# Two cleared sums take the last six blocks' rows of a sparse layer, and the other result rows are loaded meanwhile

## The reference

```python
top_w, top_idx = jax.lax.top_k(scores, TOP_K)          # TOP_K = 4, 16 experts
top_w = top_w / jnp.sum(top_w, axis=-1, keepdims=True)
g = jnp.einsum('bsh,khe->bske', x, gate_proj)          # h = 256, e = 224
u = jnp.einsum('bsh,khe->bske', x, up_proj)
act = jax.nn.silu(g) * u
out = jnp.einsum('bske,keh->bskh', act, down_proj)
sel = jnp.take_along_axis(out, top_idx[..., None], axis=2)
return jnp.sum(sel * top_w[..., None], axis=2)         # and x + this is the output
```

## Time and profile before

| | |
|---|---|
| median of three runs | 856.86 us |
| profiled execution, first to last instruction | 859.4 us |
| PE busy | 775.1 us, 90% |
| DVE busy | 554.2 us, 64% |
| ACT busy | 384.4 us, 45% |
| POOL busy | 238.3 us, 28% |
| mean granted TensorE clock | 0.956 |

### The profile page before, as it was taken

The page is one execution under the profiler, slowest core; times in us unless marked ns, Lnnn a source line. Parts: engine busy times, 40 slices in busy tenths (PEclk is TensorE's granted clock), DMA queues, the critical chain, the costliest instruction groups (busy, mean ns, idle before and its releaser), DMA issues. The chain is left out here.

```text
span 859.4 us, 15356 instructions
## 1 busy us (share of the span) xinstructions
PE 775.1 (90%) x5288; PEld 566.7 (66%) x5288; DVE 554.2 (64%) x1291; ACT 384.4 (45%) x847; POOL 238.3 (28%) x296
## 2 busy tenths in 40 slices
PE   6899878999999999997778999989989888999995
PEld 2455546878998999993335655555555537888884
DVE  3799946533432222223987999899996357888854
ACT  2466534332321111110334766666675407888860
POOL 2344420520000000004641433444431421434340
PEclk8999988999999999999899999899999798999999
DMA  9465441390289999836610001010125119999817
GB/s 337 176 245 223 189 153 56 94 405 16 78 296 387 388 345 316 304 137 158 203 34 2 25 11 45 25 51 31 46 82 208 56 42 347 411 396 393 336 56 251
DMA packets 57104, 158.03 MB, mean 184 GB/s; under 512 B 7180, under 2 KB 36748, under 8 KB 51708
## 3 DMA queue, kind: packets, MB, share of 16 engines
q1 hardware_dynamic: 51700, 141.97, 45.5%
q0 software_dynamic: 5328, 15.08, 4.9%
HBM read 114.21 MB, written 42.81 MB: 183 GB/s over the span
## 5 line engine op out<-in xcount | busy, mean ns | idle before, releaser
L1271 PEld LDWEIGHTS ps<-f_xT,f_rg 128*128 128x128 f32 x920 | 113.4, 192 | 5.2 <-DMA f_rg<-w_routed 1.7
L1271 PE MATMUL ps<-f_xT,f_rg 128*128 128x128 f32 x920 | 113.9, 275 | 1.3 <-DMA f_rg<-w_routed 1.3
L1176 DVE TENSOR_TENSOR f_rhT<-f_gate,ps 128x256 f32<-128x256 f32 (+1 forms) x69 | 25.9, 376 | 117.2 <-ACT f_gate L981 73.0
L2078 ACT ACTIVATE b_PX<-ps 128x512 f32<-128x512 f32 x128 | 72.7, 597 | 46.3 <-PE ps L2313 44.7
L1811 DVE TENSOR_REDUCE b_smax<-ps 128x4 f32<-128x1024 f32 x64 | 77.9, 1217 | 15.7 <-PE ps L2289 15.4
L981 ACT ACTIVATE f_gate<-ps 128x256 f32<-128x256 f32 (+1 forms) x69 | 24.0, 348 | 134.2 <-PE ps L1271 134.2
L2606 POOL DMA_INDIRECT y<-f_ys,f_to x47 | 45.1, 959 | 81.7 <-DVE f_to L2684 78.2
L1285 PE MATMUL ps<-f_rd,f_rhT 128*128 128x256 f32 x230 | 62.3, 387 | 0.0
L2313 PE MATMUL ps<-b_Q,b_Cx 100*128 100x256 f32 x256 | 55.8, 327 | 6.3 <-ACT b_PX L2078 6.0
L2313 PEld LDWEIGHTS ps<-b_Q,b_Cx 100*128 100x128 f32 x256 | 41.9, 206 | 26.6 <-ACT b_PX L2078 12.2
L1583 POOL MEMSET b_half<- 128x1 f32 x1 | 0.1, 99 | 212.9 <-POOLq L69 212.9
(11 more groups left out here) (333 smaller groups left out, 1843.1 us busy)
## 6 DMA issues: line engine op xcount, KB each, us to landing
f_rg<-w_routed SPq DMA_DIRECT2D x23, 1280.0 KB
rows<-a_blank SPq DMA_DIRECT2D x16, 1152.0 KB, 7.0
f_rd<-w_routed SPq DMA_DIRECT2D x23, 640.0 KB, 5.5
f_rw<-w_ffn SPq DMA_DIRECT2D x19, 704.0 KB
rw<-w_ffn SPq DMA_DIRECT2D x16, 704.0 KB
later<-w_ffn SPq DMA_DIRECT2D x12, 704.0 KB
f_xs<-rows SPq DMA_DIRECT2D x31, 144.0 KB
f_yk<-y SPq DMA_DIRECT2D x8, 512.0 KB, 7.8
```

The costliest lines, as they stand in the source:

```text
L1271: mm = nc.tensor.matmul(ps[:, u % 4, k * P:(k + 1) * P], rg[b % R_SLOTS][:, off:off + P], xT[b % 2][:, c, :], start=(c == 0), stop=(c == C ...
L2078: nc.scalar.activation(PX[g % RING][:].rearrange("p c m -> p (c m)"), ps[:, RETS + G_TURN[g] % 2, :], ACT.Exp, scale=XSC).then_inc(turn_re ...
```

## The change

Layer 1's result tensor y grows by two sums of 1024 token rows each, with 128 rows beside each for rows that hold no token (SUM_ROWS1 = 1152). In layer 0's experts stage SP clears y's first 4096 rows (4096 KB) and the two sums (2304 KB) from a zero tile. The first 41 blocks of layer 1 scatter as before. The last six (ADDED1) compute another destination: the token's row in sum b % 2, or a row beside it. POOL scatters them with an add; from the third of the six on it first waits until the scatter two blocks earlier, to the same sum, has landed. SP waits for the first 41 scatters only, loads `yk`, then waits for the others and loads the two sums of each tile (`ya`, 256 KB each). PE adds all tiles' `yk` rows 0 and 1, then all tiles' `ya` rows, into the same PSUM banks; DVE does its two adds for all tiles, then the final ones. PE's filler matmuls at the end are gone.

```diff
+ADDED1 = 6
+SUMS1 = TOP1 * TOKENS + BLOCKS1 * P
+SUM_ROWS1 = TOKENS + P
...
@@ routed_experts, SP, in the loop over the loads of chunks 4 to 9
                 sp.dma_start(raw[j % W_SLOTS][:], w_shared[j]).then_inc(w_loaded[j % W_SLOTS], 16)
+                if j == SHARED_CHUNKS - 3:
+                    sp.wait_ge(zeros_set, 1)
+                    nothing = zeros[:].bitcast(F32)
+                    first = results_dram[0:TOP1 * TOKENS].rearrange("(p n) d -> p n d", p=P)
+                    sums = results_dram[SUMS1:SUMS1 + 2 * SUM_ROWS1].rearrange("(p n) d -> p n d", p=P)
+                    for to, n in ((first, TOP1 * TOKENS // P), (sums, 2 * SUM_ROWS1 // P)):
+                        sp.dma_start(to, bc(nothing, 1, n)).then_inc(results_cleared, 16)
...
+            sp.wait_ge(results_cleared, 32)
...
@@ sparse_experts, SP
             for n in range(Y_SLOTS):
-                sp.wait_ge(y_sent[n], 16 * ((BLOCKS1 + Y_SLOTS - 1 - n) // Y_SLOTS))
+                sp.wait_ge(y_sent[n], 16 * ((BLOCKS1 - ADDED1 + Y_SLOTS - 1 - n) // Y_SLOTS))
             per_tile = y_dram[0:TOP1 * TOKENS].rearrange("(k t p) d -> t p k d", k=TOP1, p=P)
             for t in range(TILES):
                 sp.dma_start(yk[t][:], per_tile[t]).then_inc(yk_loaded[t], 16)
+            for n in range(Y_SLOTS):
+                sp.wait_ge(y_sent[n], 16 * ((BLOCKS1 + Y_SLOTS - 1 - n) // Y_SLOTS))
+            sums = y_dram[SUMS1:SUMS1 + 2 * SUM_ROWS1].rearrange("(k n) d -> n k d", k=2)
+            for t in range(TILES):
+                sp.dma_start(ya[t][:], sums[t * P:(t + 1) * P]).then_inc(ya_loaded[t], 16)
...
@@ POOL
-                pool.indirect_dma_start(y_dram, bass.IndirectOffsetOnAxis(ap=to[b % A_SLOTS][:, 0:1], axis=0), ys[b % Y_SLOTS][:], None
-                                        ).then_inc(y_sent[b % Y_SLOTS], 16)
+                at = bass.IndirectOffsetOnAxis(ap=to[b % A_SLOTS][:, 0:1], axis=0)
+                if b < BLOCKS1 - ADDED1:
+                    pool.indirect_dma_start(y_dram, at, ys[b % Y_SLOTS][:], None).then_inc(y_sent[b % Y_SLOTS], 16)
+                    continue
+                if b >= BLOCKS1 - ADDED1 + 2:
+                    pool.wait_ge(y_sent[(b - 2) % Y_SLOTS], 16 * ((b - 2) // Y_SLOTS + 1))
+                pool.indirect_dma_start(y_dram, at, ys[b % Y_SLOTS][:], None, compute_op=ALU.add).then_inc(y_sent[b % Y_SLOTS], 16)
...
@@ DVE, address(b)
+                s, n = b % 2, b - BLOCKS1 + ADDED1
+                nc.vector.tensor_copy(token[s][:], at).then_inc(token_ready, 1)
+                nc.vector.tensor_scalar(unused[s][:], at, float(TOP1 * TOKENS), beside[:, s:s + 1], ALU.is_ge, ALU.mult).then_inc(token_ready, 1)
+                dve.wait_ge(token_ready, 3 * n + 2)
+                nc.vector.tensor_scalar(token[s][:], token[s][:], TOKENS - 1, None, ALU.bitwise_and).then_inc(token_ready, 1)
+                dve.wait_ge(token_ready, 3 * n + 3)
+                nc.vector.scalar_tensor_tensor(out=to[b % A_SLOTS][:], in0=token[s][:], scalar=float(SUMS1 + s * SUM_ROWS1), in1=unused[s][:],
+                                               op0=ALU.add, op1=ALU.max).then_inc(to_ready, 1)
...
@@ DVE, before the blocks: two more columns like `nowhere`; after them: the final add in a loop of its own
+            for s in range(2):
+                nc.vector.tensor_scalar(beside[:, s:s + 1], K[:, K_PAD:K_PAD + 1], float(SUMS1 + s * SUM_ROWS1 + TOKENS - TOP1 * TOKENS), None,
+                                        ALU.add).then_inc(nowhere_set, 1)
...
+            for t in range(TILES):
                 dve.wait_ge(whole_sum, t + 1)
                 dve.wait_ge(pair_sum, t + 1)
                 nc.vector.tensor_tensor(X[:, t, :], ps[:, t, 0:D], X[:, t, :], ALU.add).then_inc(x_added, 1)
...
@@ PE, the end
-            keep_busy(24)
             pe.wait_ge(y_kept, BLOCKS1)
-            for n in range(Y_SLOTS):
-                pe.wait_ge(y_sent[n], 16 * ((BLOCKS1 + Y_SLOTS - 1 - n) // Y_SLOTS))
-            keep_busy(30)
             for t in range(TILES):
                 pe.wait_ge(yk_loaded[t], 16)
                 for k in range(2):
-                    mm = nc.tensor.matmul(ps[:, t, 0:D], ident, yk[t][:, k], start=(k == 0), stop=(k == 1))
+                    nc.tensor.matmul(ps[:, t, 0:D], ident, yk[t][:, k], start=(k == 0), stop=False, skip_group_check=True)
+            for t in range(TILES):
+                pe.wait_ge(ya_loaded[t], 16)
+                for k in range(2):
+                    mm = nc.tensor.matmul(ps[:, t, 0:D], ident, ya[t][:, k], start=False, stop=(k == 1), skip_group_check=True)
                 mm.then_inc(pair_sum, 1)
```

More of the change, by code:

```diff
@@ L119, in decoder_kernel @@
             routed_experts(nc, "f0", w_shared0, w_routed0, rows0_dram, y0_dram, X, XN, xh, xl, K, KR, ps, logits0, dest0, wk0,
-                           raw0, w0_loaded, ctx_rows, ctx_dram, blank_ctx)
+                           raw0, w0_loaded, ctx_rows, ctx_dram, blank_ctx, y1_dram)
         eb1 = whole.enter_context(nc.sbuf_tensor("eb1", [P, MORE1], mybir.dt.int32))
@@ L776, in routed_experts @@
 def routed_experts(nc, tag, w_shared, w_routed, rows_dram, y_dram, X, XN, xh, xl, K, KR, ps, logits, dest, wk, raw, w_loaded,
-                   ctx_rows, ctx_dram, blank_ctx):
+                   ctx_rows, ctx_dram, blank_ctx, results_dram):
     ctx = ExitStack()
@@ L889, in routed_experts @@
         row_set = sem("row_set")
+        results_cleared = sem("results_cleared")
         blank_stored = sem("blank_stored")
@@ L2520, in sparse_experts @@
         nowhere = sb("nowhere", [P, BLOCKS1])
+        beside = sb("beside", [P, 2])
+        token = [sb(f"token{n}", [P, 1], mybir.dt.int32) for n in range(2)]
+        unused = [sb(f"unused{n}", [P, 1]) for n in range(2)]
+        ya = [sb(f"ya{t}", [P, 2, D]) for t in range(TILES)]
         yk = [sb(f"yk{t}", [P, TOP1, D]) for t in range(TILES)]
@@ L2542, in sparse_experts @@
         yk_loaded = [sem(f"yk_loaded{t}") for t in range(TILES)]
+        ya_loaded = [sem(f"ya_loaded{t}") for t in range(TILES)]
+        token_ready = sem("token_ready")
         half_sum = sem("half_sum")
@@ L2683, in address @@
                     dve.wait_ge(y_sent[b % Y_SLOTS], 16 * (b // Y_SLOTS))
-                nc.vector.tensor_tensor(to[b % A_SLOTS][:], pick[b % A_SLOTS][:, 1:2], nowhere[:, b:b + 1], ALU.min).then_inc(to_ready, 1)
+                at = pick[b % A_SLOTS][:, 1:2]
+                if b < BLOCKS1 - ADDED1:
+                    nc.vector.tensor_tensor(to[b % A_SLOTS][:], at, nowhere[:, b:b + 1], ALU.min).then_inc(to_ready, 1)
+                    return
+                s, n = b % 2, b - BLOCKS1 + ADDED1
[6 more added lines that the diff above has]
+                                               op0=ALU.add, op1=ALU.max).then_inc(to_ready, 1)
             nc.vector.tensor_scalar(nowhere[:], KR[:, R_BLK:R_BLK + BLOCKS1], float(P), K[:, K_PAD:K_PAD + 1], ALU.mult,
                                     ALU.add).then_inc(nowhere_set, 1)
-            dve.wait_ge(nowhere_set, 1)
+            for s in range(2):
+                nc.vector.tensor_scalar(beside[:, s:s + 1], K[:, K_PAD:K_PAD + 1], float(SUMS1 + s * SUM_ROWS1 + TOKENS - TOP1 * TOKENS), None,
+                                        ALU.add).then_inc(nowhere_set, 1)
+            dve.wait_ge(nowhere_set, 3)
             dve.wait_ge(h_set, 1)
@@ L2893 @@
     rows1 = nc.dram_tensor("rows1", (SPARE1 + 1, P, ROW1), F32).ap()
-    y1 = nc.dram_tensor("y1", (TOP1 * TOKENS + BLOCKS1 * P, D), F32).ap()
+    y1 = nc.dram_tensor("y1", (SUMS1 + 2 * SUM_ROWS1, D), F32).ap()
     decoder_kernel(nc, *args, out, ctx_parts, ctx_blank, rows0, y0, rows1, y1)
```

## The result

The kernel after took 862.71 us (median of 20 runs) where the kernel before took 858.44 in 20 runs: ratio 1.0050, 95% interval 1.0031 to 1.0069, that is 4.3 us slower (2.7 to 5.9). The forecast was 858.6 against 856.86, +1.7 us, with a range of 851 to 865.

The account below looks back on a forecast made before the run. The tail bounds the kernel, with 15.56 us of `yk` loads. Of 5.9 us gain, later landing takes 4.8; slower PE sums and 2 us of low clock give 861.1 against 859.4, +1.7 us; median 858.6, range 851 to 865.

Parts of the forecast that it names:

- The `yk` loads under the blocks: End of layer 1: `yk` loads issue at 826.8, 12.1 us earlier, beside the last blocks; gain on offer 5.9 us.
- DVE's address: Late blocks: the address takes four DVE operations instead of one, ending the blocks 0.8 us later (0 to 2.2).
- The adding scatter: Last six blocks' scatters: each adding one lands in 4.3 us, the middle between 2.39 and 6.2 us for plain scatters.
- The last landing: End of layer 1: waits between scatters put the last landing at 843.6 instead of 838.8, taking 4.8 us of the 5.9.
- Rival C: Last scatters: adds are slow, 6.2 us each; first `ya` tile 853.1, end 866.0, +6.6 us; chance 0.22.
- The `ya` loads, PE and the clock: Tail: first `ya` tile 4.45 us after issue, PE bounds the sums at 7.2 us, low clock loses 2 us more.
- The clears: Layer 0: clearing 6400 KB takes 17 us from 153.4 to 170.5 on nearly idle DMA; cost 0.
- A: The forecast itself: chained adding scatters and slower PE end eat the gain; +1.7 us, range -2.5 to +4.3; chance 0.45.
- rival B: Last scatters: adds are cheap, each landing in 2.4 to 3 us, none waiting for another; -4.3 us; chance 0.28.

## Why the prediction was right, and where its sizes were off

**The `yk` loads under the blocks.** Right. Issued at 823.52, K - 8.6; forecast 826.8 against a K of 835.9, K - 9.1.

**DVE's address.** Right in kind, too dear: forecast +0.8 us, measured 0.26. A block grew by 0.12 us (2.64 for 2.52), not 0.27, though four blocks did and not three.

**The adding scatter.** This is the term that was mis-sized. Forecast 4.3 us each, beside the loads or not, from the middle of two rows of plain scatters. Measured from start to landing: 3.85 us without the loads; beside them 8.1 us for the first and 6.98 for the third. The wait for a landing costs 0.76 us more before POOL starts the next, not 0.3: the 0.30 in the earlier trace rows is the gap behind POOL's own last instruction, not the time from a release. So the starts lie 8.8 us (first to third) and 7.8 (third to fifth, 832.45 to 840.20) apart. POOL's own instruction is 1.6 us where a plain one is 0.96, which I had only named as a way to be wrong. As the plain scatters landed in 5.3 us beside the loads and in 2.4 without, and the adding ones in 7.0 to 8.1 and 3.8, the traffic is the larger part and the add the smaller: the earlier trace rows's 6.2 us, which I kept as the upper end because its neighbours were other loads, was near the plain scatter here, and the adding one lies above it. The small pieces of the `yk` loads were no help: with 4 KB pieces the adding scatters were about as slow.

**The last landing.** Forecast 843.6 with blocks ending at 835.9, so 7.7 us after K; measured 13.8 (842.08 + 3.85 - 832.16). Against 3.7 before, the change loses 10.1 us here, not 4. Taken away one at a time, the chain is worth 4.3 us, the traffic 6.9, the add 5.0; they overlap, since a chain of slow links is what is long. Rival C, with 6.2 us each, had put the landing at 848.5, 12.6 us after its K; the measured 13.8 lies beyond even that, although the chain's last link ran when the loads were over and was short. (In absolute time it is 845.93, earlier than 848.5 only because the blocks of this execution ended 3.7 us earlier than the forecast's.)

**The `ya` loads, PE and the clock.** Forecast from the last landing to the end 17.5 us (861.1 - 843.6); measured 16.0 (861.9 - 845.93), where before it was 20.6. The `ya` data came 2.75 us after issue, not 4.45: about half of the 5.19 us of a tile twice as large, where I had taken off only half of the time between two tiles. Why the first tile comes so much sooner no run shows. PE's sums took 9.04 us, forecast 9.2, without a gap: PE bounds, as said. The clock fell as said: PE idle for 8.16 us, then 0.50 until about 852.9. Its price, put at 2 us, is 1.95 (9.02 us against 7.07).

**The clears.** Right: 0, by experiment and trace, although they landed at about 179.7 (issued at 156.8, 22.9 us to landing) and not at 170.5.

The sum by these terms: +10.1 - 4.6 = +5.5 us from K, the 0.26 lying ahead of K; forecast were +4.0 - 3.1 from K and 0.8 ahead of it. The direction and the mechanism (a chain of adding scatters eats the gain) were the forecast's. The size was not: the timed +4.3 is at the upper end of A's own range, and from K to the end C's 30.1 us (866.0 - 835.9) is nearer to the measured 29.7 than A's 25.2. Of the two opposite errors (landing 6 us too early, the rest 1.5 too long) the first decided. That the number stayed so near is in part luck: the second error took 1.5 us of the first back, and the wide range, reaching to C, held the rest. The rule of the Trainium skill ("Collectives: The Full Stack", bandwidth ceiling: an add costs a second source read, no cycles) is stated there for the steps of a ring, and I had read it as speaking for rival B, cheap adds. Here an adding scatter without the loads is 1.4 us dearer than a plain one (3.80 against 2.39 to 2.43), and POOL's instruction is 0.6 us longer; whether the rest is the second read, no run shows. B was wrong.

## What to carry to other kernels

To load under the last blocks frees DMA time only if nothing that the end waits for uses the same engines: here the loads about doubled the time to landing of the scatters behind which the end stood (7.0 to 8.1 us for 3.8), and a chain of waits put two such landings one behind the other ahead of the last. Price a chain by its slowest link under the load that the change itself creates, taken from the most loaded row that the trace has: the earlier trace rows was that row, and the sum made with it came nearest. And where a transfer stands alone on the chain, look at the shape of its pieces first: one changed index order (4 KB runs for 1 KB) took 1.9 us off the load in the trace without touching the schedule.

## What the runs showed that I had not expected

An indirect DMA with an add occupies POOL for 1.56 to 1.80 us, a plain one for 0.96. Beside a stream of loads that fills the DMA engines (share 1.11), a plain 128 KB scatter landed in 5.3 us instead of 2.4, an adding one in 7 to 8 instead of 3.8. With a second queue, ACT's, the same loads took 1.3 us longer in the one trace taken (15.0 instead of 13.65 to the last use), with tiles arriving in pairs.
